# Differences of decay sums on ScalarE instead of VectorE, rows times D on VectorE instead of ScalarE

## The reference

```python
h = rmsnorm(layernorm(x), norm1_w)
z, xBC, dt = split(h @ in_proj_w)
xBC = silu(causal_conv(xBC));  xs, Bm, Cm = split(xBC)
dA = softplus(dt + dt_bias) * A                # A < 0
A_cum = cumsum(dA)                             # within a chunk, per head
L = exp(A_cum[l] - A_cum[s]) for l >= s, else 0
Y_diag = (Cm Bm^T * L) @ (xs * dt)
Y_off  = exp(A_cum) * (Cm @ state)             # state from the chunks before
y = Y_diag + Y_off + D_param * xs              # D_param: one number per head
y = rmsnorm(y * silu(z), mixer_norm_w)
h1 = x + y @ out_proj_w;  out = h1 + mlp(rmsnorm(h1))
```

## Time and profile before

| | us |
|---|---|
| median of 3 runs (735.88 to 762.37) | 739.1 |
| the profiled execution | 738.58 |
| its span, first to last instruction | 736.8 |
| busy in the span: TensorE | 694.8 (94%) |
| VectorE | 585.6 (79%) |
| ScalarE | 237.8 (32%) |
| GpSimd | 246.1 (33%) |

### The profile page before, as it was taken

The page is one execution under the profiler, slowest core; times in us unless marked ns, Lnnn a source line. Parts: engine busy times, 40 slices in busy tenths (PEclk is TensorE's granted clock), DMA queues, the critical chain, the costliest instruction groups (busy, mean ns, idle before and its releaser), DMA issues.

```text
span 736.8 us, 10028 instructions
## 1 busy us (share of the span) xinstructions
PE 694.8 (94%) x2867; PEld 447.6 (61%) x2868; DVE 585.6 (79%) x1427; ACT 237.8 (32%) x480; POOL 246.1 (33%) x395
## 2 busy tenths in 40 slices
PE   5978979999999989999988999999999999999996
PEld 4445665568556756775884666666665555656564
DVE  3899989977868584477786888888888888888883
ACT  1576747586376345223102111111111111111110
POOL 2133442524322342320003233333333343434323
PEclk8999979999999999999999999999999999999999
DMA  9133000200040045023106883111133352525112
GB/s 318 58 112 116 0 1 1 115 0 1 31 143 1 1 148 209 1 85 123 58 0 202 298 283 73 28 29 28 28 93 114 78 138 59 148 48 174 29 16 28
DMA packets 37271, 63.00 MB, mean 86 GB/s; under 512 B 3376, under 2 KB 26992, under 8 KB 37232
## 3 DMA queue, kind: packets, MB, share of 16 engines
q1 hardware_dynamic: 29744, 52.54, 20.6%
q0 software_dynamic: 7488, 9.97, 8.1%
HBM read 52.73 MB, written 9.76 MB: 85 GB/s over the span
## 4 chain that ended last, share of the span: by engine, by line
PE 74%; DVE 15%; issue 3%; POOL 3%; ACT 3%; DMA 2%; DVEq 0%; POOLq 0%; ACTq 0%
PE ps L1077 25%; PE ps L1098 12%; PE ps L745 4%; PE ps L757 4%; PE ps L771 4%; PE ps L439 3%; PE ps L1086 3%; PE ps L494 3%; PE ps L561 3%; DVE big L1642 2%; PE ps L711 2%; DVE big L1662 2%; PE ps L618 2%; PE ps L508 2%; DVE big L2238 2%
## 5 line engine op out<-in xcount | busy, mean ns | idle before, releaser
L2238 DVE STREAM_TRANSPOSE big<-big 32x224 f32<-32x224 f32 x560 | 225.4, 403 | 8.4
L1077 PE MATMUL ps<-big 128*128 x512 | 198.3, 540 | 1.3 <-ACT big L1543 0.7
L1077 PEld LDWEIGHTS ps<-big 128*128 128x128 f32 x512 | 96.8, 190 | 87.9 <-issue 86.6
L1098 PE MATMUL ps<-big 128*128 x448 | 102.2, 380 | 1.0 <-DVE big L2238 0.6
L1549 ACT ACTIVATE big<-ps 128x896 f32<-128x896 f32 x36 | 33.0, 917 | 200.7 <-PE ps L1077 177.5
L2286 POOL TENSOR_TENSOR big<-big 128x1 f32<-128x1 f32 x110 | 38.4, 349 | 163.4 <-DVE big L2247 143.1
L1098 PEld LDWEIGHTS ps<-big 128*128 128x128 f32 x448 | 82.7, 190 | 11.7 <-issue 1.8
L2254 DVE TENSOR_TENSOR big<-big,ps 128x896 f32<-128x896 f32 x36 | 39.1, 1088 | 41.0 <-PE ps L1077 36.4
L439 PEld LDWEIGHTS ps<-big 128*128 128x128 f32 x319 | 39.5, 144 | 37.5 <-issue 26.3
L439 PE MATMUL ps<-big 128*128 128x128 f32 x319 | 51.8, 277 | 7.9 <-ACT big L1180 2.3
L1642 DVE SCALAR_TENSOR_TENSOR big<-ps,big 128x511 f32<-128x511 f32 (+2 forms) x72 | 52.9, 746 | 6.2 <-ACT big L1199 4.4
(11 more groups left out here) (224 smaller groups left out, 1037.9 us busy)
## 6 DMA issues: line engine op xcount, KB each, us to landing
big<-in_w SPq DMA_DIRECT2D x36, 896.0 KB, 7.4
big<-cum_rows SPq DMA_DIRECT2D x16, 512.0 KB, 5.4
out_rows<-big SPq DMA_DIRECT2D x4, 512.0 KB, 2.9
xn_rows<-big SPq DMA_DIRECT2D x4, 512.0 KB, 3.2
big<-in_hidden SPq DMA_DIRECT2D x1, 1536.0 KB, 12.6
big<-in_in_proj SPq DMA_DIRECT2D x1, 1288.0 KB, 7.5
big<-in_gate SPq DMA_DIRECT2D x1, 640.0 KB, 13.1
big<-in_up SPq DMA_DIRECT2D x1, 640.0 KB, 8.2
```

What stands on the lines that cost most here:

```text
L1077: last = mm(bank(bk + n)[:, 0:HALF], xT[:, k, :], expert_cols(e, off + k * M + n * HALF, HALF), start=(k == 0), stop=(k == KD - 1))
L1098: last = mm(bank(7)[:, 0:D], hTs[:, half, j * P:(j + 1) * P], expert_cols(e, 2 * KD * M + j * D, D), start=(j == 0), stop=(j == MB - 1))
L2238: last = V.transpose(hTs[c * SQ:(c + 1) * SQ, half, :].rearrange("p (j t) -> p j t", j=MB)[:, :, q * SQ:(q + 1) * SQ], ha[q * SQ:(q + 1) * ...
```

## The change

`apart` goes away on VectorE. ScalarE stores `cums` negated, and `decay` first takes, for each of the 8 heads, the absolute value of `em` plus that bias (128 columns each), raises `apart_ready`, waits for it, and exponentiates the 1024 columns with a scale of -1. For l >= s this is the same number; elsewhere it is a positive decay that the mask of `scores` removes. `decay` itself now waits for the sums and for the spread transfer of its chunk. `x_D` goes away on ScalarE and becomes one VectorE product of 512 columns with D broadcast over each head's 64 columns. The places of `decay` in ScalarE's order stay; VectorE's order loses 32 `apart` steps and gets 16 `x_D` steps at places of its own, such as ahead of `scores(0, 0)`, `scores(0, 2)`, `hT1(2)` and `scores(2, 1)`. TensorE's, GpSimd's and SyncE's orders stay.

```diff
@@ ScalarE, dec_e and decay
-                    act.wait_ge(apart_ready, n * CH * 2)
+                    act.wait_ge(apart_ready, n * CH)
-                A(cums..., bank(MISC)[...], ACT.Copy).then_inc(cums_taken, 1)
+                A(cums..., bank(MISC)[...], ACT.Copy, scale=-1.0).then_inc(cums_taken, 1)
...
             def decay(n, c):
-                act.wait_ge(apart_ready, 2 * nth(n, CH, c))
-                A(em[n % 2][:, c, :], em[n % 2][:, c, :], ACT.Exp).then_inc(decays, 1)
+                act.wait_ge(cums_taken, n + 1)
+                act.wait_ge(cum_in[c], 16 * (n + 1))
+                for hh in range(HEADS):
+                    q = slice(hh * P, (hh + 1) * P)
+                    last = A(em[n % 2][:, c, q], em[n % 2][:, c, q], ACT.Abs, bias=cums[:, c, hh:hh + 1])
+                last.then_inc(apart_ready, 1)
+                act.wait_ge(apart_ready, nth(n, CH, c))
+                A(em[n % 2][:, c, :], em[n % 2][:, c, :], ACT.Exp, scale=-1.0).then_inc(decays, 1)
...
-            def x_D(n, c):                       # ScalarE, 16 calls in its order go too
-                for hh in range(HEADS):
-                    q = slice(hh * HD, (hh + 1) * HD)
-                    last = A(xsd[:, c % 2, q], xs[:, q], ACT.Copy, scale=vec[:, V_D + hh:V_D + hh + 1])
-                last.then_inc(xsd_ready, 1)
@@ VectorE
-            def apart(n, c, part):               # 32 calls in its order go too
-                v.wait_ge(cums_taken, n + 1)
-                v.wait_ge(cum_in[c], 16 * (n + 1))
-                for hh in range(part * HEADS // 2, (part + 1) * HEADS // 2):
-                    q = slice(hh * P, (hh + 1) * P)
-                    last = V.tensor_scalar(em[n % 2][:, c, q], em[n % 2][:, c, q], cums[:, c, hh:hh + 1], 0.0, ALU.subtract, ALU.min)
-                last.then_inc(apart_ready, 1)
+            def x_D(n, c):
+                v.wait_ge(xs_taken, nth(n, CH, c))
+                if n * CH + c >= 2:
+                    v.wait_ge(y4_ready, n * CH + c - 1)
+                V.tensor_tensor(heads(xsd[:, c % 2, :]), heads(xs), over_head(vec[:, V_D:V_D + HEADS]), ALU.mult).then_inc(xsd_ready, 1)
@@ VectorE's order, parts of it
-            apart(0, 0, 0)
             masked_G(0)
-            apart(0, 0, 1)
             ln1_stats(2)
             hT1(1)
+            x_D(0, 0)
             scores(0, 0)
-            apart(0, 1, 0)
-            apart(0, 1, 1)
-            apart(0, 2, 0)
-            apart(0, 2, 1)
             scores(0, 1)
-            apart(0, 3, 0)
-            apart(0, 3, 1)
             dt_abs_(1)
             state(0, 0)
             conv_taps(1, 0)
+            x_D(0, 1)
             scores(0, 2)
             dt_softplus(1)
             off(0, 1)
 
             y_(0, 0)
             conv_taps(1, 1)
+            x_D(0, 2)
             conv_taps(1, 2)
...
             y_(0, 3)
             h1_(0, 2)
+            x_D(1, 0)
             hT1(2)
             scores(1, 0)
-            apart(1, 2, 0)
-            apart(1, 2, 1)
-            apart(1, 3, 0)
+            x_D(1, 1)
             dt_abs_(2)
...
             add_mlp(0, 0)
             add_mlp(0, 1)
+            x_D(2, 0)
             scores(2, 1)
```

More of the change, by code:

```diff
@@ L1189, in dec_e @@
                     act.wait_ge(cum_out, 16 * n)
-                    act.wait_ge(apart_ready, n * CH * 2)
+                    act.wait_ge(apart_ready, n * CH)
                 A(cumT[0:CH * HEADS, :], bank(MISC)[0:CH * HEADS, M_CUM:M_CUM + P], ACT.Copy).then_inc(cumT_taken, 1)
-                A(cums.rearrange("p a b -> p (a b)"), bank(MISC)[:, M_DT + CH * HEADS:M_DT + 2 * CH * HEADS], ACT.Copy).then_inc(cums_taken, 1)
+                A(cums.rearrange("p a b -> p (a b)"), bank(MISC)[:, M_DT + CH * HEADS:M_DT + 2 * CH * HEADS], ACT.Copy, scale=-1.0).then_inc(cums_taken, 1)
                 A(dec[n % 2].rearrange("p a b c -> p (a b c)"), bank(MISC)[:, M_DT:M_DT + 3 * CH * HEADS], ACT.Exp).then_inc(dec_taken, 1)
@@ L1220, in bt_copy @@
                 A(bt.rearrange("p a b -> p (a b)"), bank(TURN0), ACT.Copy).then_inc(bt_taken, 1)
-            def x_D(n, c):
-                act.wait_ge(xs_taken, nth(n, CH, c))
-                if n * CH + c >= 2:
-                    act.wait_ge(y4_ready, n * CH + c - 1)
-                for hh in range(HEADS):
-                    q = slice(hh * HD, (hh + 1) * HD)
-                    last = A(xsd[:, c % 2, q], xs[:, q], ACT.Copy, scale=vec[:, V_D + hh:V_D + hh + 1])
-                last.then_inc(xsd_ready, 1)
             def z_silu(n, t):
@@ L1324, in _ @@
             hT0(1)
-            x_D(0, 0)
             decay(0, 1)
@@ L1338, in _ @@
             yT_copy(0, 0)
-            x_D(0, 1)
             square_y(0, 0)
@@ L1349, in _ @@
             conv_silu(1, 3)
-            x_D(0, 2)
             front(0, 3)
@@ L1357, in _ @@
             z_silu(1, 2)
-            x_D(0, 3)
             z_silu(1, 3)
@@ L1366, in _ @@
             front(1, 0)
-            x_D(1, 0)
             front(1, 1)
@@ L1377, in _ @@
             tap(2, 2)
-            x_D(1, 1)
             tap(2, 3)
@@ L1408, in _ @@
             square_y(1, 1)
-            x_D(1, 2)
             front(1, 3)
@@ L1420, in _ @@
             square_y(1, 2)
-            x_D(1, 3)
             gate(0, 5)
@@ L1430, in _ @@
             dt_e(3)
-            x_D(2, 0)
             tap(3, 0)
@@ L1451, in _ @@
             conv_silu(3, 4)
-            x_D(2, 1)
             front(2, 2)
             conv_silu(3, 5)
-            x_D(2, 2)
             z_silu(3, 3)
@@ L1471, in _ @@
             gate(1, 3)
-            x_D(2, 3)
             bt_copy(3)
@@ L1476, in _ @@
             front(3, 0)
-            x_D(3, 0)
             yT_copy(2, 2)
@@ L1489, in _ @@
             square_h(2, 3)
-            x_D(3, 1)
             decay(3, 3)
@@ L1499, in _ @@
             front(3, 2)
-            x_D(3, 2)
             route_exp(0)
@@ L1511, in _ @@
             gate(2, 5)
-            x_D(3, 3)
             logits_copy(1)
@@ L1991, in _ @@
             scores(0, 3)
-            apart(1, 0, 0)
-            apart(1, 0, 1)
             state(0, 2)
             y_(0, 2)
+            x_D(0, 3)
             masked_G(1)
-            apart(1, 1, 0)
             ln1_h(2)
@@ L2001, in _ @@
             h1_(0, 1)
-            apart(1, 1, 1)
             y_(0, 3)
             h1_(0, 2)
+            x_D(1, 0)
             hT1(2)
             scores(1, 0)
-            apart(1, 2, 0)
-            apart(1, 2, 1)
-            apart(1, 3, 0)
+            x_D(1, 1)
             dt_abs_(2)
-            apart(1, 3, 1)
             dt_softplus(2)
@@ L2029, in _ @@
             state(1, 1)
+            x_D(1, 2)
             scores(1, 2)
             scores(1, 3)
[L2032 to L2036, removed]
             hidden_(0, 0)
@@ L2043, in _ @@
             h1_(1, 0)
+            x_D(1, 3)
             y_(1, 2)
@@ L2048, in _ @@
             hidden_(0, 2)
-            apart(2, 2, 1)
-            apart(2, 3, 0)
-            apart(2, 3, 1)
             scores(2, 0)
@@ L2071, in _ @@
             conv_taps(3, 0)
+            x_D(2, 1)
             add_mlp(0, 2)
@@ L2086, in _ @@
             state(2, 1)
+            x_D(2, 2)
             hidden_(1, 0)
-            apart(3, 0, 0)
             y_(2, 1)
             h1_(2, 0)
-            apart(3, 0, 1)
-            apart(3, 1, 0)
-            apart(3, 1, 1)
             off(2, 2)
-            apart(3, 2, 0)
-            apart(3, 2, 1)
-            apart(3, 3, 0)
             hidden_(1, 1)
@@ L2103, in _ @@
             hidden_(1, 2)
+            x_D(2, 3)
             hidden_(1, 3)
             h1_(2, 1)
-            apart(3, 3, 1)
             masked_G(3)
+            x_D(3, 0)
             scores(3, 0)
@@ L2115, in _ @@
             y_(2, 3)
+            x_D(3, 1)
             h1_(2, 2)
@@ L2138, in _ @@
             route_weigh(0)
+            x_D(3, 2)
             hidden_(2, 1)
@@ L2144, in _ @@
             hidden_(2, 3)
+            x_D(3, 3)
             hidden_(2, 4)
```

## The result

The changed kernel took 763.04 us (median of 4 runs, 760.79 to 764.71), the kernel before beside it 738.9: a ratio of 1.0333, 95% interval 1.0303 to 1.0363. The change makes the kernel 3.3% slower. (Of the four runs of the kernel before, one of 762.37 us is a slow one and is left out of the ratio.) The profiled execution took 762.2 with a span of 760.4, 23.6 more than before.

What follows compares the result with a forecast made beforehand. VectorE was taken to set the pace from 38 to 104 us and TensorE after, with hand-written order deciding. Shifts along ScalarE's serial chain summed to +13.0 on 738.6, giving 751.6, put at 752 us; range 738 to 764.

Steps and rivals of the forecast that it cites:

- the walk: Follows the engines' hand-written orders from 42 us on, adding up shifts to +13.0 us; with bounds, 745 to 760 us.
- the spells of low clock: Rival: new TensorE waits near 64, 101 and 135 us bring more 1.2 GHz spells, 2 to 5 us each; chance 0.24.
- further spells at half: Sign of a wrong forecast: the granted clock shows more spells at half than before.
- Prices: ScalarE: absolute value 0.39 us, eight in 2.44; VectorE: product 0.72 us, 16 in 11.5; removed: 34.9 VectorE, 32.2 ScalarE.
- The rival of a table of its own: Absolute value needs an unloaded ScalarE table: 16 loads of 1.28 us, eight in the serial chain, +10, 762 us; chance 0.04.
- 42 to 62 us: Four decays become one serial ScalarE chain; copy for chunk 1 ends at 60.0, VectorE's scores(0,2) shifts +4.2 us.
- 62 to 104 us: Product for chunk 2 and its wait make +6; two TensorE waits go, hT(2) +3.7; ScalarE's decay(1,0) makes dt_(2) +4.8.
- four products by +1.07: Part of the bounds on the sum: four of VectorE's new products each take 1.07 us more.
- step of 137 to 161 us: Decay(2,0) and decay(2,1) on ScalarE stand ahead of needed work, 0.7 and 1.5 us seen: shift +9.5, bounds 7.4 to 12.3.
- 104 to 203 us: Later ScalarE decays delay TensorE: +7.4 at h2T, +9.5 by 161 us, then +12.7 through the product ahead of scores(2,1).
- The relief wins: Rival: VectorE is the bound to 104 us, so TensorE's 11.05 us of idle time there come back: 728 us; chance 0.12.

Runs made afterwards that it cites:

- the kernel with fillers: The changed kernel with extra TensorE products of 128x256, results unused, put at five of TensorE's waits; 752.99 us (ratio 1.0191).
- the control: The kernel before, differences and products unmoved, with ScalarE's order for sequence 0 rearranged: hT0(1) ahead of the first exponential, front(0, 1) ahead of the third; 743.0 us.

## Why the prediction was right or wrong

The range held the time (738 to 764, at its very end, 1 us inside) and the main mechanism held: a serial list on ScalarE, paid in pushes. That the range held is partly luck. The sum was too small, +13.0 against +23.6 in span; the walk's own bounds, 745 to 760, missed 763; and the likeliest verdict, "same" at 0.50, was not the one measured. The wide range held because it took in the spells of low clock, as a rival. By the prediction's own words, further spells at half were a sign of its being wrong, and three came. The walk, milestone by milestone, as shift against before; the last column is the kernel with fillers, from the same starting row:

| milestone (start before, us) | forecast | changed kernel | with fillers |
|---|---|---|---|
| copy for chunk 1 (54.92) | +4.6 | +5.2 | |
| scores(0,2) (56.55) | +4.2 | +4.8 | |
| diag(0,2) (77.10) | +6 | +9.3 | |
| hT(2) (94.71) | +3.7 | +6.5 | |
| dt_(2) (99.61) | +4.8 | +7.7 | +7.9 |
| h2T(0) (129.47) | +7.4 | +10.7 | +9.7 |
| out(1,2) (160.48) | +9.5 | +14.5 | +11.8 |
| xbc at 201.36 | +12.7 | +21.4 | +16.7 |
| end of span | +13.0 | +23.6 | +17.3 |

- **Prices: right.** Abs 0.390 for 0.39, eight in 2.43 for 2.44; product 0.756 for 0.72; table loads nine and nine. The first eight Abs ran ahead of the load at 45.43 us and the next ones behind it. The rival of a table of its own falls. By that the Trainium skill, page "ScalarE: Activation LUTs", section "Table sets: the hidden batching unit", is borne out for abs here: no load stands in that group. The collisions did come, but hardly on the product: at 60.76 it took 0.69 us, while GpSimd's product of the same rows took 1.55 for 1.04 and the scores behind it 2.07 for 1.22.
- **42 to 62 us: right.** The chain came out 0.7 longer than worked out, with the one gap of 0.72 for the tap, which the sum had at nothing.
- **62 to 104 us: the first step that failed.** "A wait for its copy ... (1 to 2 us, I take 1.2): +6" came out as +9.3 at diag(0,2). Two terms were mis-sized. The product for chunk 2 waited 3.06 us; and scores(0,2), which I let run in 1.22, took 2.07, beside GpSimd's product of the same rows, which began at 60.81, and the operation behind it. That pushed the softplus behind it and with it the decay sums of sequence 1 to +5.7 (68.47 for 62.79), and the granted clock was 0.57 from 69 to 73. The rest of the step held: from diag(0,2) to hT(2) TensorE took 14.8 us, for the 15.3 forecast, so the two waits for VectorE did go.
- **The product's place in general.** My price list had it as a length (0.7) or "nothing"; the walk let it wait for its copy in places, and sized such a wait once (1.2 us for chunk 2, which came out at 3.06). Alone it costs 14 us (the run with the product alone), nearly as much as the Abs alone (17.5). In the changed kernel VectorE waits 23.6 us ahead of it in all; with eight of them moved down, 13 us came back. The sum of the waits is not the price, though: 13.2 us of them go with 14 us of time in the kernel with the product alone, 13.4 with 6 to 9 where VectorE has room. The range's bound "four products by +1.07" missed the waits. It is missing from its own sum as well: with it the listed bounds add up to 28 at the upper end, not 24, which is what they make without it. (In the step of 137 to 161 us, 0.7 and 1.5 make +9.6, not +9.5, which changes nothing.)
- **104 to 203 us: right where the clock was held.** I forecast 2.6, 2.1 and 3.2 for the three pushes; with fillers they are 1.7, 2.2 and 4.8, in the changed kernel 3.0, 3.8 and 6.9. The first two fit the chain and the clock without another cause; the third is larger, as in both kernels the product ahead of scores(2,1) waited 3.3 (at 195.04 in the changed one) and the scores behind it ran 4.05 for two, where before had 3.19.
- **The clock was no rival but a term.** I gave it 0.24 as another way to go, at 759 to 761 with two spells more. It came on top of the chain, with three: 6.3 us by the traces, 10 by the medians. So, by the traces, of the 10.6 us above my sum about 4 remain with the fillers (3.1 of them are there by dt_(2), the waits and collisions just named) and about 6 go with the clock. The two are not separate in the kernel: the run with VectorE's list mended lost 7 us less of clock without a filler.
- **The relief wins: it did not.** Even with nothing added to either engine it gives 733; 728 is the edge of that interval. VectorE's 34.9 us were worth 6 to 9.
- Left open: why fillers don't bring the shift below 17 us, and how the extra clock loss of the Abs alone (20.5 us of lost clock at 756) divides into its waits. Nor was the Abs in its new places run with the products left on ScalarE.

## What to carry to other kernels

Moving work from a busy engine to an idle one moves it into that engine's list: walk the list, not the sums of busy time, and where that engine sets the pace, ask of an inserted instruction what it waits for while other work stands behind it. Split a step so that the part with early inputs can go into a gap: the same operations (two table loads apart) cost 24 us in the old order and, reordered on both engines, came out nearly 4 us under the kernel before. Count new pauses of TensorE ahead of time as part of each push: here the spells at 48, 69, 106, 140 and 198 us began near the ends of pauses of 4.16, 3.92, 2.28, 2.92 and 2.18 us.

## What the runs showed of the hardware

- Small VectorE operations with SBUF operands stretched beside GpSimd as large ones did: the 128x32 add that opens the softplus took 1.25 us at 63.36 in the changed kernel, beside a GpSimd operation of 2.25 that began at 62.32, and 0.17 in the kernel with both lists mended, where GpSimd had ended:

```profile
58.02 0.17 DVE L1618 TENSOR_SCALAR big<-big 128x32 f32<-128x32 f32 x1
```

  Eight subtractions took 4.27 us beside three GpSimd operations in the control, and 1.65 with GpSimd idle. So an earlier copy can slow VectorE, by moving GpSimd's work beside VectorE's; how much of the control's 4 us that is was not separated.
- Lost clock and time do not go one for one. Fillers in the changed kernel gave back 10.3 us of clock, with 10 us of time by the medians and 6.3 by the traces; in the kernel with both lists mended they gave back 6.8 us of clock and no time (735.9 without, 736.97 with). The kernel with the product alone lost as much clock as the changed kernel, 18.8 us, and is 10 us faster.
